# Row maxima to the softmax shift row by DMA instead of by TensorE in a decoder layer

## The reference

```python
qw = (q_in @ Wq + bq).reshape(B, M, HEADS, QSIZE)
kw = (k_in @ Wk + bk).reshape(B, N, HEADS, QSIZE)
vw = (v_in @ Wv + bv).reshape(B, N, HEADS, KSIZE)
a = jnp.einsum('bmhd,bnhd->bhmn', qw, kw) / jnp.sqrt(jnp.float32(QSIZE))
a = jnp.where(key_mask[:, None, None, :], a, -jnp.inf)
a = jax.nn.softmax(a, axis=-1)
o = jnp.einsum('bhmn,bnhd->bmhd', a, vw).reshape(B, M, HEADS * KSIZE)
return o @ Wo + bo
```

## Time and profile before

| | |
|---|---|
| median of 3 runs | 1361.86 us (1358.66 to 1362.01) |
| profiled execution, its own time | 1363.67 us |
| its span, first to last instruction | 1361.9 us |
| mean granted clock of TensorE | 0.979 |
| PE busy | 1303.6 us (96%) |
| DVE busy | 919.2 us (67%) |
| ACT busy | 829.2 us (61%) |
| POOL busy | 771.8 us (57%) |
| DMA | 42.85 MB, mean 31 GB/s |

### The profile page before, as it was taken

The page is one execution under the profiler, slowest core; times in us unless marked ns, Lnnn a source line. Parts: engine busy times, 40 slices in busy tenths (PEclk is TensorE's granted clock), DMA queues, the critical chain, the costliest instruction groups (busy, mean ns, idle before and its releaser), DMA issues.

```text
span 1361.9 us, 20879 instructions
## 1 busy us (share of the span) xinstructions
PE 1303.6 (96%) x7056; PEld 880.7 (65%) x7056; DVE 919.2 (67%) x1803; ACT 829.2 (61%) x1122; POOL 771.8 (57%) x447
## 2 busy tenths in 40 slices
PE   5999979999999999999999999999999998899995
PEld 4767756667566656666666666657566665577773
DVE  5678876674766676566747656674765677678885
ACT  2344436675666576665757665675666666678883
POOL 3504227885777687667948767694876787300000
PEclk8999989999999999999999999999999999899997
DMA  6211220000100100010010001000100100111100
GB/s 209 96 45 62 80 79 1 1 1 1 65 1 1 64 0 0 0 64 0 0 58 6 0 0 64 0 0 15 48 0 0 63 1 1 34 45 47 46 32 31
DMA packets 25535, 42.85 MB, mean 31 GB/s; under 512 B 3440, under 2 KB 7936, under 8 KB 25488
## 3 DMA queue, kind: packets, MB, share of 16 engines
q1 hardware_dynamic: 24672, 39.10, 8.4%
q0 software_dynamic: 816, 3.15, 0.7%
HBM read 29.66 MB, written 12.58 MB: 31 GB/s over the span
## 4 chain that ended last, share of the span: by engine, by line
PE 87%; DVE 4%; ACT 3%; POOL 2%; issue 2%; SPq 1%; DMA 1%; POOLq 0%; ACTq 0%; DVEq 0%
PE ps L1276 15%; PE ps L1253 14%; PE ps L48 10%; PE ps L50 10%; PE ps L49 9%; PE ps L1261 4%; PE ps L1255 4%; PE ps L1267 2%; PE ps L1309 2%; PE ps L1310 2%; PE ps L1308 2%; PE ps L1620 2%; PE ps L1621 2%; PE ps L1285 2%; PE ps L721 1%
## 5 line engine op out<-in xcount | busy, mean ns | idle before, releaser
L1118 DVE CUSTOM_DVE_ANT_0 junk<-ps,mask 128x512 bf16<-128x512 f32 x512 | 319.9, 687 | 94.2 <-PE ps L1261 92.7
L977 ACT ACTIVATE prob<-ps,mcol 128x1024 f32<-128x1024 f32 x256 | 282.1, 1116 | 138.8 <-PE ps L1255 134.8
L905 POOL TENSOR_TENSOR acc<-acc,prob 128x1024 f32<-128x1024 f32 x128 | 306.5, 2395 | 11.5
L902 POOL TENSOR_TENSOR acc<-prob 128x1024 f32<-128x1024 f32 x64 | 153.9, 2404 | 227.6 <-ACT prob L977 226.6
L1276 PE MATMUL ps<-prob,v_b 128*64 128x512 f32 x1024 | 244.5, 598 | 0.0
L919 POOL TENSOR_TENSOR acc_lo<-acc,acc_hi 128x1024 f16<-128x1024 f32 x64 | 138.9, 2170 | 5.1
L1276 PEld LDWEIGHTS ps<-prob,v_b 128*64 128x64 f32 x1024 | 67.8, 136 | 107.9 <-issue 73.6
L1123 DVE TENSOR_TENSOR ps<-ps,recip 128x512 f32<-128x512 f32 x64 | 44.8, 699 | 120.3 <-ACT recip L992 120.3
L1253 PE MATMUL ps<-q_hi,k_hi 64*128 64x512 f32 x512 | 115.2, 446 | 4.6 <-DVE rs L226 2.8
L1261 PE MATMUL ps<-k_hi,q_hi 64*128 64x512 f32 x512 | 103.1, 399 | 8.3 <-DVE nmx L1118 5.6
L1255 PE MATMUL ps<-shift,ones_r 64*128 64x512 f32 x512 | 102.6, 396 | 0.0
(11 more groups left out here) (213 smaller groups left out, 2972.4 us busy)
## 6 DMA issues: line engine op xcount, KB each, us to landing
x_in<-in_xT SPq DMA_DIRECT2D x8, 512.0 KB, 3.7
x_scratch<-x_a SPq DMA_DIRECT2D x8, 512.0 KB, 2.8
raw<-in_cT SPq DMA_DIRECT2D x8, 512.0 KB, 5.7
raw<-x_scratch SPq DMA_DIRECT2D x8, 512.0 KB, 4.8
y<-x_scratch SPq DMA_DIRECT2D x8, 512.0 KB, 3.8
y_scratch<-y SPq DMA_DIRECT2D x8, 512.0 KB, 2.8
y_c<-y_scratch SPq DMA_DIRECT2D x8, 512.0 KB, 4.1
outT<-x SPq DMA_DIRECT2D x8, 512.0 KB, 2.8
```

Source lines behind the costliest of these rows:

```text
L902: pool.tensor_tensor(total, prob[:, 0], prob[:, 1], ALU.add).then_inc(acc_out, 1)
L905: pool.tensor_tensor(total, total, prob[:, kt], ALU.add).then_inc(acc_out, 1)
L977: act.activation(prob[:, i].rearrange("p h t -> p (h t)"), SCORE[i % 2].rearrange("p h t -> p (h t)"), ACT.Exp, scale=SCALE, bias=mcol[:, ...
L1118: dve.tensor_tensor_reduce(junk[:, t % 2, h], SMAX[t % 2][:, h], mask[:], -1.0, -LOWEST, ALU.add, ALU.min, nmx[:, t, h * DH:h * DH + 1]).t ...
```

## The change

The maxima are written densely: `nmx` becomes [128, 2, 2, 4] (pair parity, head, query tile), so each partition holds the four maxima of a head side by side, 16 bytes. ACT issues two DMAs for each pair, one for each head (`maxima_to_rows`), that take these 128 pieces of 16 bytes to partition 0 or 64 of the shift row, one piece behind the other. The row is therefore ordered query first and tile second, and the shift matmul reads it with a step of four elements (16 bytes) to get the queries in order. The four identity matmuls, the identity itself and its load, and ACT's copy are gone. The shift row gets two buffers, by pair parity, each with a semaphore of its own. It is cleared once by POOL (128x1024, where `nmx`, 128x512, was cleared before), later in POOL's stream. ACT's two DMAs stand straight behind the exponentials and wait for all 8 maxima of the next pair. TensorE keeps its wait for these maxima ahead of `keys`, and waits for the row no longer ahead of the first key tile's products but ahead of its shift matmul.

```diff
--- before.py
+++ after.py
@@ -87,7 +87,6 @@
         c = {}
         c["mean_w"] = sb(whole, "mean_w", [P, P], F32)
         c["ones_w"] = sb(whole, "ones_w", [P, P], F32)
-        c["ident"] = sb(whole, "ident", [P, P], F32R)
         c["eps"] = sb(whole, "eps", [P, 1], F32)
         c["wfc"] = sb(whole, "wfc", [P, DK, HID], F32)
         c["tern"] = sb(whole, "tern", [P, HK, D], BF16)
@@ -293,7 +292,6 @@
         w_hi[w] = sb(ctx, w + "_l0_hi", [P, DK, D], F32R)
         w_lo[w] = sb(ctx, w + "_l0_lo", [P, DK, D], F32R)
     stage = c["raw"][:].rearrange("p k i t -> p k (i t)")
-    ident_f = sb(ctx, "ident_f", [P, P], F32)
     bits = sb(ctx, "bits", [P, 6, P], F32)
     nbit = sb(ctx, "nbit", [P, P], F32)
     decay = sb(ctx, "decay", [P, 6], F32)
@@ -342,7 +340,6 @@
         sp.dma_start(decay[:, 5:6], a["log_decay"][:, 0:1].partition_broadcast(P)).then_inc(decay_in, 16)
         load_weight("WoT", w_in)
         load_weight("WvT", w_in)
-        sp.dma_start(ident_f[:], a["ident"]).then_inc(consts_in, 16)
         sp.dma_start(bits[:], a["bits"]).then_inc(consts_in, 16)
         sp.dma_start(x[:, 1], batch_cols(a["xT"], 1)).then_inc(x_in[1], 16)
         sp.dma_start(wfc[:], a["wfcT"].rearrange("(k p) n -> p k n", p=P)).then_inc(f_in, 16)
@@ -499,9 +496,8 @@
         dve.wait_ge(w_in, 32)
         split_weight(2, "WoT", raw["WoT"][:])
 
-        dve.wait_ge(consts_in, 32)
+        dve.wait_ge(consts_in, 16)
         dve.wait_ge(sig_done, 1)
-        dve.tensor_copy(c["ident"][:], ident_f[:]).then_inc(setup, 1)
         dve.tensor_copy(dmask[:], bits[:, 5, :]).then_inc(pow_step, 1)
         n = 1
         for j in range(5):
@@ -804,15 +800,16 @@
     acc_hi = sb(ctx, "acc_hi", [P, 2, T], F16)
     prob = sb(ctx, "prob", [P, NT, 2, T], F32)
     junk = sb(ctx, "junk", [P, 2, 2, T], BF16)
-    shift = sb(ctx, "shift", [P, T], F32R)
-    sb(ctx, "spare", [P, DK, T], F32)
+    shift = sb(ctx, "shift", [P, 2, T], F32R)
+    sb(ctx, "spare", [P, T + 2 * P], F32)
     v = sb(ctx, "v_b", [P, NT, HD], F32)
     q_hi, q_lo, k_hi, k_lo = (sb(ctx, n, [P, 2, T], F32R) for n in ("q_hi", "q_lo", "k_hi", "k_lo"))
     mask_u8 = sb(ctx, "mask_u8", [P, T], U8)
     mask = sb(ctx, "mask", [P, T], F32)
     mcol_u8 = sb(ctx, "mcol_u8", [P, NT], U8)
     mcol = sb(ctx, "mcol", [P, NT], F32)
-    nmx = sb(ctx, "nmx", [P, NT, P], F32R)
+    sb(ctx, "spare_end", [P, NT, P - 4], F32)
+    nmx = sb(ctx, "nmx", [P, 2, 2, NT], F32R)
     ones_r = sb(ctx, "ones_r", [P, P], F32R)
     ones_h = sb(ctx, "ones_h", [P, DH], F16)
     wo = c["wo"]
@@ -823,7 +820,7 @@
     x_rounded, x_split, c_rounded, c_split = sem("x_rounded"), sem("x_split"), sem("c_rounded"), sem("c_split")
     q_ps, q_hi_out, q_lo_out = sem("q_ps"), sem("q_hi_out"), sem("q_lo_out")
     k_ps, k_hi_out, k_lo_out = sem("k_ps"), sem("k_hi_out"), sem("k_lo_out")
-    smax_ps, nm_out, row_ps, row_out = sem("smax_ps"), sem("nm_out"), sem("row_ps"), sem("row_out")
+    smax_ps, nm_out, row_in = sem("smax_ps"), sem("nm_out"), [sem("row_in_even"), sem("row_in_odd")]
     st_ps, exp_out, pv_ps, pvc_out, acc_out = sem("st_ps"), sem("exp_out"), sem("pv_ps"), sem("pvc_out"), sem("acc_out")
     sum_hi_out, sum_lo_out = sem("sum_hi_out"), sem("sum_lo_out")
     den_ps, log_out, recip0_out = sem("den_ps"), sem("log_out"), sem("recip0_out")
@@ -836,7 +833,7 @@
     SCORE = (ps[:, 0:2, :], ps[:, 2:4, :])
     SMAX = (ps[:, 4:6, :], ps[:, 6:8, :])
     FIRST_KEY, FIRST_QUERY = (ps[:, 2, :], ps[:, 3, :]), (ps[:, 6, :], ps[:, 0, :])
-    PV, ROW, KEY, QUERY, DEN = ps[:, 0, :], ps[:, 1, :], ps[:, 2, :], ps[:, 6, :], ps[:, 3, :]
+    PV, KEY, QUERY, DEN = ps[:, 0, :], ps[:, 2, :], ps[:, 6, :], ps[:, 3, :]
     VAL = (ps[:, 4, :], ps[:, 5, :])
     OUT = (ps[:, 4, :], ps[:, 7, :])
 
@@ -949,7 +946,6 @@
                     pool.wait_ge(q_ps, PAIRS * B)
                     f.ternary(pool)
 
-        pool.memset(f32(nmx[:]), 0.0).then_inc(consts, 1)
         pool.memset(f32(ones_r[:]), 1.0).then_inc(consts, 1)
         pool.memset(ones_h[:], 1.0).then_inc(consts, 1)
         pool.wait_ge(la.raw_in, 32)
@@ -957,6 +953,8 @@
         split_c(0)
         pool.tensor_copy(x_hi[:], raw_x).then_inc(x_rounded, 1)
         split_x(0)
+        pool.wait_ge(la.gate_used, B)
+        pool.memset(f32(shift[:]), 0.0).then_inc(consts, 1)
         split_output_weight()
         batch(0, True, False)
         with pool.Fori(1, B - 1) as b:
@@ -999,9 +997,11 @@
                 act.wait_ge(o_ps, 2 * DK * b)
             act.activation(att_hi[:, p % HALF], DEN, ACT.Identity, bias=c["bv"][:, p:p + 1]).then_inc(att_hi_out, 1)
 
-        def shift_row(g):
-            act.wait_ge(row_ps, g + 1)
-            act.activation(shift[:], ROW, ACT.Copy).then_inc(row_out, 1)
+        def maxima_to_rows(g, p):
+            act.wait_ge(nm_out, 8 * g + 8)
+            for h in range(2):
+                act.dma_start(f32(shift[h * DH:h * DH + 1, p % 2]),
+                              f32(nmx[:, p % 2, h])).then_inc(row_in[p % 2], 16)
 
         def keys_hi(g, p, bank=KEY):
             act.wait_ge(k_ps, g + 1)
@@ -1036,6 +1036,8 @@
                 p2 = (p + 2) % PAIRS
                 for i in range(NT):
                     exps(b, g, i, head)
+                if nxt:
+                    maxima_to_rows(g + 1, (p + 1) % PAIRS)
                 if p == PAIRS - 2 and not last:
                     round_x(b + 1)
                 if last and p == HALF - 2:
@@ -1045,8 +1047,6 @@
                 if not head:
                     reciprocal_estimate(g - 1, first and p == 1)
                 values_copied(g, p % 2, first and p < 2)
-                if nxt:
-                    shift_row(g + 1)
                 if first and p == 1:
                     act.wait_ge(la.stored, 16 * B)
                 if p > 0:
@@ -1075,7 +1075,8 @@
         values_out(0, (3, 4, 5))
         la.deviation_last()
         values_out(0, (6, 7))
-        shift_row(0)
+        act.wait_ge(consts, 3)
+        maxima_to_rows(0, 0)
         batch(0, True, False)
         with act.Fori(1, B - 1) as b:
             batch(b, False, False)
@@ -1116,7 +1117,7 @@
                     dve.reg_add(tiles_scored, tiles_scored, 1)
                 for h in range(2):
                     dve.tensor_tensor_reduce(junk[:, t % 2, h], SMAX[t % 2][:, h], mask[:], -1.0, -LOWEST, ALU.add,
-                                             ALU.min, nmx[:, t, h * DH:h * DH + 1]).then_inc(nm_out, 1)
+                                             ALU.min, nmx[:, p % 2, h, t:t + 1]).then_inc(nm_out, 1)
 
         def reciprocal(g):
             dve.wait_ge(recip0_out, g + 1)
@@ -1247,12 +1248,14 @@
             if kt == 0:
                 pe.wait_ge(k_lo_out, g + 1)
                 pe.wait_ge(q_lo_out, g + 1)
-                pe.wait_ge(row_out, g + 1)
             for n, (l, r) in enumerate(((k_hi, q_hi), (k_lo, q_hi), (k_hi, q_lo))):
                 for h in range(2):
                     pe.matmul(banks[:, h], l[OWN[h], par, cols], r[OWN[h], par], start=(n == 0), stop=False)
+            if kt == 0:
+                pe.wait_ge(row_in[par], 16 * (g - par) + 32)
             for h in range(2):
-                mm = pe.matmul(banks[:, h], ones_r[OWN[h], :], shift[OWN[h], :], start=False, stop=True)
+                rows = shift[OWN[h], par].rearrange("d (q t) -> d t q", t=NT)
+                mm = pe.matmul(banks[:, h], ones_r[OWN[h], :], rows, start=False, stop=True)
             mm.then_inc(st_ps, 1)
 
         def max_scores(g, p, t):
@@ -1260,12 +1263,6 @@
             for h in range(2):
                 mm = pe.matmul(SMAX[t % 2][:, h], q_hi[OWN[h], par, toks], k_hi[OWN[h], par], start=True, stop=True)
             mm.then_inc(smax_ps, 1)
-
-        def maxima_to_row(g):
-            pe.wait_ge(nm_out, 8 * g + 8)
-            for t in range(NT):
-                mm = pe.matmul(ROW[:, t * P:(t + 1) * P], nmx[:, t, :], c["ident"][:], start=True, stop=True)
-            mm.then_inc(row_ps, 1)
 
         def weighted_values(g, p, tiles):
             for kt in tiles:
@@ -1360,7 +1357,7 @@
                 if last and p == PAIRS - 2:
                     f.var2_first(pe)
                 if nxt:
-                    maxima_to_row(g + 1)
+                    pe.wait_ge(nm_out, 8 * g + 16)
                 if nxt2:
                     b2 = b if p < PAIRS - 2 else b + 1
                     keys(b2, g + 2, p2)
@@ -1401,7 +1398,6 @@
             max_scores(0, 0, t)
         pe.wait_ge(consts, 3)
         pe.wait_ge(bo_centred, 1)
-        maxima_to_row(0)
         batch(0, True, False)
         with pe.Fori(1, B - 1) as b:
             batch(b, False, False)
@@ -1692,7 +1688,7 @@
         "bv": columns(i["L0_xattn_bv"]),
         "fast_bT": i["L0_ffn_fast_b"].T, "wfcT": i["L0_ffn_w_fc"].T, "wprojT": i["L0_ffn_w_proj"].T,
         "uT": i["L0_ffn_u"].T, "v": i["L0_ffn_v"], "gate": i["L0_ffn_gate"].reshape(1, 1),
-        "ident": np.eye(P, dtype=np.float32), "bits": bits,
+        "bits": bits,
```

## The result

The changed kernel takes **1398.96 us** (median of 4 runs, 1397.29 to 1400.12) against 1361.62 for the kernel before in the same comparison (1358.66 to 1362.01): a ratio of **1.028**, 95% interval 1.0266 to 1.0294. It is 37.3 us slower. The prediction had the sign right and the size wrong: 1375 was forecast, and 1399 lies above the range of 1346 to 1387.

A forecast was written before the change was run, and what follows sets the result against it. TensorE was taken to bound the kernel (87% of the chain), ACT once a batch. Plain pairs 1.9, batch ends 10.2 and first landing 0.5 sum to 12.6, about +13, forecasting 1375 us; range 1346 to 1387.

The forecast's parts named there:

- What bounds the kernel: Cross attention: a microsecond of TensorE is one of the kernel, except pair 6, where ACT's chain already bounds once a batch.
- The slot of 0.44: Slot for both heads' shift matmuls with the stepped read: 0.44 us, a doubling of 0.23, chosen between DVE's ratio and difference.
- Net for a plain pair: +0.03 to 0.04: Plain pair on TensorE: -0.50 for removed matmuls, +0.84 for longer slots, -0.31 for waits replaced.
- 0.31 of waits: Plain pair: TensorE waits the longer slots replace, 0.21 for the first exponential and 0.10 ahead of the weighted values.
- The 0.10 ahead of the weighted values: TensorE ahead of the weighted values: 0.10 us taken as a lost wait (765.37 against 765.47) that goes.
- The removed matmuls: Four identity matmuls ahead of keys: 0.50 us a pair on the path, 64 times, minus 32.0 us.
- 10.2 of the forecast's +13: Batch ends: ACT's issues delay pairs 6 and 7 by 1.45 us together, at seven batch ends, 10.2 us.
- The DMAs on ACT: Two issues a pair ahead of the reciprocal, 0.44 us each (bounds 0.1 and 0.54), costing only at the end of a batch.
- hidden in a plain pair: Plain pair: reciprocal 0.63 later, yet q_hi ends by 13.5 where TensorE wants it at 13.68.
- The landing, POOL's clearing, the removed copy: Landing under 4 us, hidden, except 0.5 once in the first pair; POOL's clearing and ACT's removed copy: nothing.
- The step costs more: Rival, shift-matmul slot 0.59: plain pair 0.6 longer, +49, 1411 us; at a slot of 0.93, +131; chance 0.08.
- The step is free: Rival, shift-matmul slot stays 0.23: 13.4 us gained in all, 1348 us, faster; chance 0.28.

The follow-up runs named there:

- e2: The kernel before with one edit: its single contiguous shift row read with a step of four elements, no DMA added, no matmul removed; 1405.98 us, ratio 1.0323.
- e4: The changed kernel with the row DMAs issued by SP in place of ACT, stepped read kept; 1380.00 us, ratio 1.0134 to before.
- e5: The changed kernel with DMAs issued by SP and the step moved from the shift matmul's read to the weight load of max_scores; 1340.51 us, ratio 0.9846 to before.
- e9: The changed kernel with round_x (bx_hi) put ahead of ACT's two DMA issues in the pair before a batch's last; 1394.51 us, ratio 1.0243 to before.
- e1: The changed kernel with shift matmuls reading the row contiguously, without the step, queries out of order; 1365.83 us, ratio 1.0036 to before.

## Why the prediction was wrong

**What bounds the kernel: right.** TensorE's microseconds were the kernel's. e2 adds work to no engine but TensorE, and its plain pairs are longer by 0.76.

**The slot of 0.44: right, and it was a choice.** The doubling stands in the changed kernel, in e2 and with a step of 8 bytes. DVE's rows had the direction, and the point between their ratio and their difference came out, but a doubling is what the runs show, not what those rows implied; that the choice hit it is in part luck. The Trainium skill's page "Advanced Engine Details and Errata" (section Memory Cachelines, SBUF Cachelines) speaks of 16-byte lines and of at least two hits on a line for full speed. The trace agrees that a step of 16 bytes has a penalty; it does not agree on the threshold, since a step of 8 bytes, with two columns in 16 bytes, lasts 612 ns against 618.

**"Net for a plain pair: +0.03 to 0.04": this step failed.** e4 shows it alone: +0.25 to 0.32 in each pair but pair 6, seven of them 2.07 a batch, and with pair 6 (+0.58) 2.65, 21 us in eight batches, where I had 1.9 us for pairs 0 to 5. Three errors make it up.
- The slot behind a stepped read is 0.26 and not 0.23: 0.03 four times, 0.12. The sum had no such term.
- Of the 0.31 of waits that the longer slots were to absorb, the 0.21 for the first exponential did go (749.02, 749.28, 749.52 follow each other by 0.26 and 0.24). The 0.10 ahead of the weighted values was no wait: 751.80 to 752.15 is 0.35, as long as before (0.33), although TensorE arrives later, and in e5 it is 721.55 to 721.89, 0.34. A fixed step at the change from the 64-row matmuls to the 128-row ones was read as a wait. Together, 0.84 + 0.12 − 0.21 = 0.75, and e2 measured 0.76.
- The removed matmuls gave 0.45 and not 0.50. They start 0.50 ahead of `keys`, but in e2, which still has them, the first matmul of `keys` is followed after 0.28, and without them after 0.34 (756.16 to 756.50). I read it as a cost of about 0.05 for the first matmul of a new group, which falls on `keys` when the identity matmuls are gone; no run takes it apart.

```profile
750.90 0.45 PE L48 MATMUL ps<-bc_hi,wk_hi 128*128 128x512 f32 x1
751.18 0.39 PE L49 MATMUL ps<-bc_lo,wk_hi 128*128 128x512 f32 x1
```

0.76 − 0.45 = 0.31, which is 0.27 above the forecast's 0.04: 0.12 + 0.10 + 0.05. A difference between two terms of about 0.5 each was carried to 0.01, with errors of 0.23 in one and 0.05 in the other, and multiplied by 64.

The sign came out right for only a part of its reason: 10.2 of the forecast's +13 stood on ACT's issues, while the step, less the removed matmuls, already makes the kernel 18 us slower without any issue on ACT (e4).

**The DMAs on ACT: right that they cost at the end of a batch, wrong in price and in place.** Two issues took 1.25 and not 0.88; 0.54 each had been the upper bound, and the medians are 582 ns on ACT and 515 on SP against the 428 of the earlier trace rows. The reciprocal began 8.73 into pair 3 where 8.13 was forecast. The issues have only 0.48 of that lateness: in e4, without them, it begins 8.25 in (748.06 − 739.81), because the longer slots make the sums that it reads later, which the forecast did not count. From both follow the 0.14 to 0.26 in pairs 2 to 4: `q_hi`, "hidden in a plain pair" with 0.2 of slack, was not. TensorE's waits for it, over the kernel:

```profile
PEld ps L1264 <- ACT q_hi L1012: 27.5, 39, 1.5
...
PEld ps L48 <- POOL bx_lo L920: 7.9, 7, 1.2
```

I had followed `bx_hi` only on ACT, as something that delays the reciprocal, and expected pair 6 to be 0.5 and pair 7 0.95 longer. The consumer of `bx_hi` was not followed: POOL's `bx_lo`, then `queries`. It came to 1.94 in pair 6, of which e9 takes back 1.05, and 0.38 in pair 7. By e4 the issues cost 2.0 in a middle batch, 16 us in eight, and 4 more in the last batch, ahead of the feed-forward block, where I had looked for nothing; by the two medians 19. I had 10.2.

**The landing, POOL's clearing, the removed copy: nothing, as said.** The first pair's wait for the row was 3.0 on TensorE, but it is no loss: the first shift matmul starts 2.7 behind the last maximum (199.48 to 202.20), where the way over the identity matmuls took 3.4 (203.38 to 206.81). The 0.5 counted for it was not paid.

**The rivals.** *The step costs more* came nearer (1411) for the wrong reason: the slot was not 0.59. (Its +131 for a slot of 0.93 does not follow from the terms: 2.80 − 0.50 − 0.31 is 1.99 a pair, which makes about +138.) *The step is free* was false. In hindsight the missing rival was the forecast with its own plain pair off by the errors of its terms: 0.27 more in 64 pairs is 17 us, at 1392, outside the range.

| term, us per batch | predicted | measured | by |
|---|---|---|---|
| stepped read, plain pair | 0.53 | 0.76 | e2 |
| removed matmuls, plain pair | −0.50 | −0.45 | e4 and e2 |
| both, over a batch | 0.24 | 2.65 | e4 |
| issues on ACT, over a batch | 1.45 | 2.0 | after and e4 |
| sum | 1.69 | 4.67 | after |

## What to carry to other kernels

A stepped moving operand doubled the price of its matmul (512 columns of fp32r in 0.44 us instead of 0.23), while the same step in the weight load was hidden; if an order must be mended, mend it on the side whose load is covered. A DMA issue is an instruction of the engine that gives it, here 0.6 us: put it where that engine waits anyhow, and follow the consumers of everything behind it over the other engines, up to the one that bounds. Before a small gap in a timeline is counted as recoverable, look whether its releaser ended inside it; here the gap where the two matmul shapes meet kept a median of 0.32 to 0.36 in four traces, and none of it came back.

## What the hardware showed that I had not expected

- The price of a stepped moving read does not grow with the step: slots of 0.44, 0.44 and 0.41 for steps of 8, 16 and 32 bytes, matmul durations of 612, 618 and 587 ns in the median, against 393 contiguous in e1.
- The slot behind a stepped read is longer too, 0.26 instead of 0.23.
- A weight load of 64x128 fp32r with a step of 16 bytes takes 307 ns instead of 187, under cover of the matmul before it.
- Issuing a DMA of 128 pieces of 16 bytes holds ACT for 476 ns at least, 582 in the median, and two of them for 1.25 us until its next instruction; on SP the median is 515. Their whole queue moved 0.27 MB in 18432 packets and took 0.7% of the DMA engines' time: the price of small pieces lay in the issue, not in the transfer.
